# A token tower layer in fp32r on one core: scores in four strips, stationary router weights, a new order of the instruction lists, and the first block's sums over positions by identity matmuls

## The reference

```python
h = take(table, x)                                   # (8, 1024, 256)
h = h + attn(layernorm(h))                           # 16 heads of 16, over the FIRST axis: 8 positions
h = h + ffn(layernorm(h))
# attn: q, k, v = x @ Wqkv.T + b; softmax(q k / 4) over the 8 positions; out = (p v) @ Wo.T + bo
# ffn: s = sigmoid(x @ Wg.T), 16 experts in 4 groups; the best 2 groups, in them the best 4 experts,
#      their s normalised, times 2.5; out = sum_e w_e * relu(x @ W1[e].T)^2 @ W2[e].T
#      + relu(x @ Ws1.T)^2 @ Ws2.T                   # hidden 128 per expert, 256 shared
```

## Time and profile before

| what | value |
|---|---|
| median of 3 runs | 1297.22 us (1296.58 to 1298.70) |
| the profiled execution | 1296.51 us, span from first to last instruction 1294.7 us |
| granted TensorE clock, mean | 0.995 |
| TensorE busy | 1259.3 us, 97% |
| VectorE busy | 1022.7 us, 79% |
| ScalarE busy | 591.2 us, 46% |
| GpSimd busy | 500.2 us, 39% |
| DMA | 91.66 MB, 71 GB/s in the mean |

### The profile page before, as it was taken

One profiled execution on the slowest core, in us unless ns is written; L12 is line 12 of the kernel. 1 busy time (PEld: TensorE's weight loads), 2 busy tenths in 40 slices (PEclk: granted clock), 3 DMA queues, 4 the chain that ended last, 5 costly groups with the idle time before them and its releaser, 6 DMA issues.

```text
span 1294.7 us, 19965 instructions
## 1 busy us (share of the span) xinstructions
PE 1259.3 (97%) x7556; PEld 1037.6 (80%) x7556; DVE 1022.7 (79%) x1732; ACT 591.2 (46%) x1040; POOL 500.2 (39%) x717
## 2 busy tenths in 40 slices
PE   4798999999999999999999999999999999999998
PEld 3467889797888979788797888979788797888987
DVE  4989787887878789787878878788787878978754
ACT  5234445444554544454353544544355354444443
POOL 6437254161623507253260724416262360705100
PEclk9899999999999999999999999999999999999999
DMA  6002222121321212122121322212122120212131
GB/s 217 1 17 83 66 83 82 35 82 49 99 66 55 94 33 97 52 83 82 34 86 45 100 66 82 71 46 82 50 89 76 51 92 29 94 49 83 66 107 57
DMA packets 34128, 91.66 MB, mean 71 GB/s; under 512 B 4720, under 2 KB 13296, under 8 KB 34032
## 3 DMA queue, kind: packets, MB, share of 16 engines
q1 hardware_dynamic: 30960, 81.99, 19.0%
q0 software_dynamic: 3072, 8.39, 2.5%
HBM read 81.46 MB, written 8.91 MB: 70 GB/s over the span
## 4 chain that ended last, share of the span: by engine, by line
PE 94%; DVE 3%; issue 1%; ACT 1%; POOL 1%; DMA 0%; DVEq 0%; POOLq 0%; SPq 0%
PE psY L1157 32%; PE psH L1142 30%; PE psB L1188 10%; PE psB L1203 9%; PE psA L1233 4%; PE psB L1221 2%; PE psA L1221 2%; PE psA L1245 2%; PE psB L1174 1%; PE psA L1174 1%; DVE ring L771 1%; PE psA L1254 1%; PE psY L1261 0%; DVE stats L754 0%; POOL xin L399 0%
## 5 line engine op out<-in xcount | busy, mean ns | idle before, releaser
L1157 PE MATMUL psY<-w_hi,hid_hi 128*128 128x256 f32 x1152 | 328.5, 285 | 0.0
L1157 PE MATMUL psY<-w_hi,hid_lo 128*128 128x256 f32 x1152 | 324.5, 282 | 0.0
L1157 PE MATMUL psY<-w_lo,hid_hi 128*128 128x256 f32 x1152 | 323.6, 281 | 0.0
L733 DVE SCALAR_TENSOR_TENSOR r_sb<-psH,cwB 128x512 f32<-128x512 f32 x256 | 174.8, 683 | 113.7 <-PE psH L1142 102.9
L533 ACT ACTIVATE hid_hi<-r_sb 128x512 fp32r<-128x512 f32 x288 | 179.8, 624 | 181.4 <-PE psY L1157 181.4
L1157 PEld LDWEIGHTS psY<-w_hi,hid_hi 128*128 128x128 f32 x1152 | 217.3, 189 | 31.4 <-issue 23.5
L1142 PE MATMUL psH<-xT_hi,w_hi 128*128 128x512 f32 x576 | 229.2, 398 | 1.4 <-DVE r_sb L733 1.4
L1142 PE MATMUL psH<-xT_hi,w_lo 128*128 128x512 f32 x576 | 227.4, 395 | 0.0
L1142 PE MATMUL psH<-xT_lo,w_hi 128*128 128x512 f32 x576 | 227.3, 395 | 0.0
L531 ACT ACTIVATE p_sb<-r_sb 128x512 f32<-128x512 f32 x288 | 180.2, 626 | 101.8 <-DVE r_sb L733 94.6
L1157 PEld LDWEIGHTS psY<-w_lo,hid_hi 128*128 128x128 f32 x1152 | 216.9, 188 | 8.1
(11 more groups left out here) (136 smaller groups left out, 1980.6 us busy)
## 6 DMA issues: line engine op xcount, KB each, us to landing
cwB<-cw_dram SPq DMA_DIRECT2D x128, 512.0 KB, 3.9
out<-h SPq DMA_DIRECT2D x32, 256.0 KB, 3.2
xin<-table,idx POOLq DMA_INDIRECT x64
ring<-w_t SPq DMA_DIRECT2D x4, 256.0 KB, 5.3
h<-w_t SPq DMA_DIRECT2D x2, 512.0 KB, 8.5
ring<-w_t SPq DMA_DIRECT2D x1, 512.0 KB, 5.9
p_sb<-w_t SPq DMA_DIRECT2D x2, 256.0 KB
cwB<-w_t SPq DMA_DIRECT2D x1, 512.0 KB
```

The costliest lines, as they stand in the source:

```text
L733: nc.vector.scalar_tensor_tensor(r_sb[:, n % 2, :], psH[:, n % 2, :], 0.0, cwB[:, (r // QN) % 2, r % QN, :], ALU.max, ALU.mult).then_inc(w ...
L1157: last = nc.tensor.matmul(psY[:, j // 2, (j % 2) * D:(j % 2 + 1) * D], hid[a][:, e % R, j * P:(j + 1) * P], W2[b][:, e, :], start=(e == 0 ...
```

## The change

It has five parts.

1. **Scores.** A slot's number now is t = 2 lp + ih, and `score(blk, lp)` issues the four strips of both halves in one go: four matmuls into four different strips of 32 partitions. There are four calls of it in place of eight, in a period in two groups, (0, 1) and (2, 3), as there were two groups of four slots before.
2. **Router.** The router's weights, high and low, and Wo's high part share one tile. `logits` loads 128 columns of it (32 of the router, 96 of Wo whose results nobody reads) and streams the tokens: 4 matmuls of 512 columns. The result, 32 x 512, is copied out by ScalarE (`logits_out`, into cwT, which now has 32 rows), and `logits_back` brings it with 4 transposes to where `router` reads it.
3. **Sums of block 0.** For blk == 0 the sum over the key positions is made by `part_sum`: eight f32 matmuls with the identity, added up in psY, which the experts don't use yet. `attention_hi`/`_lo` of block 0 read psY. VectorE and GpSimd have no sums for block 0. In later blocks nothing changes here.
4. **Start part.** The second gather goes to right behind the first, ahead of the constants and of rstd_of(0, 0); warm groups, weight pieces and the calls of blocks 0 and 1 are laid out anew on all four lists.
5. **Periods.** The calls are the same but for the new ones, in a new order on TensorE, VectorE and ScalarE; on GpSimd only bias_in moves up.

The core of the diff:

```diff
         W2 = [sb(f"w2_{p}", [P, X_ALL, D], f32r) for p in ("hi", "lo")]
         WQKV = [sb(f"wqkv_{p}", [P, KH, 6, P], f32r) for p in ("hi", "lo")]
-        WO = [sb(f"wo_{p}", [P, KH, D], f32r) for p in ("hi", "lo")]
-        WG = sb("wg_hi_lo", [P, KH, 2, E], f32r)
+        WGO = sb("wg_hi_lo_wo_hi", [P, KH, 2 * E + D], f32r)
+        WO = [WGO[:, :, 2 * E:2 * E + D], sb("wo_lo", [P, KH, D], f32r)]
 
...
 
-        SUMS_VECTOR = ((1, 3, 5, 7), (3, 7))
+        SUMS_VECTOR = (3, 7)
 
         QKV_ORDER = [(0, 0), (1, 0), (0, 1), (1, 1), (2, 0), (2, 1)]
         QKV_SB = [q_sb, k_sb, v_sb]
@@ -272,7 +275,7 @@
         def product_on(eng, ns, blk, t):
 
 
-            lp, ih = t % LP, t // LP
+            lp, ih = t // KH, t % KH
             if lp == 0:
                 eng.wait_ge(qkv_ready, nth(blk, 6, 2 * (ih + 1)))
             if blk == 0 and t == 0:
@@ -289,13 +292,14 @@
 
         def summer(blk, t):
 
-            on_vector = t in SUMS_VECTOR[min(blk, 1)]
-            mine = [u for u in range(SLOTS) if (u in SUMS_VECTOR[min(blk, 1)]) == on_vector]
-            before = sum(1 for b in range(blk) for u in range(SLOTS) if (u in SUMS_VECTOR[min(b, 1)]) == on_vector)
-            return int(on_vector), before + mine.index(t), mine.index(t)
+            on_vector = t in SUMS_VECTOR
+            mine = [u for u in range(SLOTS) if (u in SUMS_VECTOR) == on_vector]
+            return int(on_vector), (blk - 1) * len(mine) + mine.index(t), mine.index(t)
 
         def wait_sum(eng, blk, t):
-            if blk >= 0:
+            if blk == 0:
+                eng.wait_ge(part_mm, t + 1)
+            elif blk > 0:
                 who, k, _at = summer(blk, t)
                 eng.wait_ge(o_ready[who], k + 1)
 
...
                     gather(b + 3)
+                if b + 2 < B:
+                    bias_in(b + 2)
                 if b + 1 < B:
                     root_of_sum(b + 1)
                 if b + 2 < B:
                     sum_of(b + 2, 0)
                     sum_of(b + 2, 1)
-                    bias_in(b + 2)
 
             link(nc.gpsimd.memset(half_neg[:, :], -0.5))
             link(nc.gpsimd.memset(ident[:, :], 0.0))
...
 
+            gather_first(1)
+            rstd_of(0, 0)
             constants_small()
-            rstd_of(0, 0)
             constants_spread()
-            gather_first(1)
             rstd_of(0, 1)
-            sum_of(0, 0)
             bias_in(0)
-            sum_of(0, 2)
-            sum_of(0, 4)
-            sum_of(0, 6)
             rstd_of(1, 0)
             gather(2)
+            bias_in(1)
             root_of_sum(0)
             sum_of(1, 0)
             sum_of(1, 1)
-            bias_in(1)
             for b in range(B + 1):
                 period(b)
...
                 wait(act, h_mm, (blk - 1) * X_ALL)
-                nc.scalar.copy(xT2[blk % 2][0][:, ih, :], o_sb[:, ih, :]).then_inc(o_hi, 1)
+                src = psY if blk == 0 else o_sb
+                nc.scalar.copy(xT2[blk % 2][0][:, ih, :], src[:, ih, :]).then_inc(o_hi, 1)
+
+            def logits_out(blk):
+                act.wait_ge(logit_mm, nth(blk, 1, 1))
+                wait(act, cwT_stored, nth(blk, 16, 0))
+                nc.scalar.copy(cwT[:, :], psA[0:2 * E, 0, :]).then_inc(lgT_ready, 1)
 
             def router(blk):
-                act.wait_ge(logit_mm, nth(blk, 1, 1))
+                act.wait_ge(lg_back, nth(blk, 1, 1))
                 wait(act, route_step, nth(blk, ROUTE_STEPS, 0))
                 nc.scalar.copy(lg[:, :, :, :].rearrange("p a b c -> p (a b c)"),
-                               psA[:, 0, 0:TT * 2 * E]).then_inc(lg_ready, 1)
+                               psA[:, 1, 0:TT * 2 * E]).then_inc(lg_ready, 1)
...
@@ -1190,19 +1209,21 @@
                                                 stop=(kh == KH - 1 and (a, b) == PASSES[-1]))
                 last.then_inc(qkv_mm, 1)
 
-            def score(blk, t):
-
-                lp, ih = t % LP, t // LP
-                pe.wait_ge(prod_ready[ih], nth(blk, LP, lp + 1))
-                if t == 0:
+            def score(blk, lp):
+
+                for ih in range(KH):
+                    pe.wait_ge(prod_ready[ih], nth(blk, LP, lp + 1))
+                if lp == 0:
                     if blk == 0:
                         pe.wait_ge(const_step, CONST_SMALL)
                     pe.wait_ge(qkv_ready, nth(blk, 6, 5))
-                for li in range(2):
-                    row = 64 * ih + 32 * li
-                    last = nc.tensor.matmul(psB[row:row + 32, 0, :], head_sum[:, lp, :], ring[:, t % 4, li, :],
-                                            start=(lp == 0), stop=(lp == LP - 1))
-                last.then_inc(score_mm, 1)
+                for ih in range(KH):
+                    for li in range(2):
+                        row = 64 * ih + 32 * li
+                        last = nc.tensor.matmul(psB[row:row + 32, 0, :], head_sum[:, lp, :],
+                                                ring[:, (KH * lp + ih) % 4, li, :],
+                                                start=(lp == 0), stop=(lp == LP - 1))
+                    last.then_inc(score_mm, 1)
 
             def spread_probs(blk, t):
 
...
@@ -1222,6 +1243,16 @@
                                             start=True, stop=True)
                 last.then_inc(spread_mm, 1)
 
+            def part_sum(t):
+
+                pe.wait_ge(av_ready, t + 1)
+                a = ring[:, t % 4, :, :].rearrange("p l (m n) -> p l m n", m=L)
+                ih, lp = t // LP, t % LP
+                for m in range(L):
+                    last = nc.tensor.matmul(psY[:, ih, 2 * lp * NN:(2 * lp + 2) * NN].rearrange("p (l n) -> p l n", l=2),
+                                            ident[:, :], a[:, :, m, :], start=(m == 0), stop=(m == L - 1))
+                last.then_inc(part_mm, 1)
+
             def out_projection(blk):
                 if blk == 0:
...
                 pe.wait_ge(xT_lo[1], nth(blk, 1, 1))
                 x = xT2[blk % 2]
+                for kh in range(KH):
+                    for a in range(2):
+                        last = nc.tensor.matmul(psA[:, 0, :], WGO[:, kh, 0:P], x[a][:, kh, :],
+                                                start=(kh == 0 and a == 0), stop=(kh == KH - 1 and a == 1))
+                last.then_inc(logit_mm, 1)
+
+            def logits_back(blk):
+                pe.wait_ge(lgT_ready, nth(blk, 1, 1))
                 for j in range(TT):
-                    for kh in range(KH):
-                        for a in range(2):
-                            last = nc.tensor.matmul(psA[:, 0, j * 2 * E:(j + 1) * 2 * E],
-                                                    x[a][:, kh, j * P:(j + 1) * P],
-                                                    WG[:, kh, :, :].rearrange("p a e -> p (a e)"),
-                                                    start=(kh == 0 and a == 0), stop=(kh == KH - 1 and a == 1))
-                last.then_inc(logit_mm, 1)
+                    last = nc.tensor.transpose(psA[:, 1, j * 2 * E:(j + 1) * 2 * E], cwT[:, j * P:(j + 1) * P],
+                                               ident[0:2 * E, 0:2 * E])
+                last.then_inc(lg_back, 1)
 
             def weights_transpose(blk):
                 pe.wait_ge(route_step, nth(blk, ROUTE_STEPS, ROUTE_STEPS))
```

More of the change, by code:

```diff
@@ L626, in period @@
                     square(b, 8)
+                    square(b, 9)
                 if b + 2 < B:
@@ L639, in period @@
                     qkv_out(b + 2, 2)
+                    qkv_out(b + 2, 3)
+                if b + 1 < B:
+                    logits_out(b + 1)
                 if b < B:
-                    square(b, 11)
                     square(b, 12)
+                if b + 2 < B:
+                    qkv_out(b + 2, 4)
                 if b + 1 < B:
@@ L972, in period @@
                 if b < B:
-                    hidden_lo(b, 11)
+                    weigh(b, 12)
+                if b + 2 < B:
+                    product(b + 2, 2)
+                    product(b + 2, 3)
+                if b < B:
                     hidden_lo(b, 12)
@@ L1005, in period @@
                 if b + 1 < B:
-                    route(b + 1, 10)
+                    route(b + 1, 5)
+                    route(b + 1, 6)
+                    route(b + 1, 7)
+                    route(b + 1, 8)
+                if b < B:
+                    weigh(b, 14)
+                if b + 1 < B:
+                    route(b + 1, 9)
+                if b < B:
+                    hidden_lo(b, 13)
+                    weigh(b, 15)
+                if b + 1 < B:
+                    route(b + 1, 10)
+                if b < B:
+                    hidden_lo(b, 14)
+                if b + 1 < B:
+                    route(b + 1, 11)
+                if b + 2 < B:
+                    scores_max(b + 2)
+                if b < B:
+                    hidden_lo(b, 15)
+                if b + 1 < B:
+                    route(b + 1, 12)
```

(76 more changed lines are left out.)

251 lines of the change are left out of this document (113 added, 138 removed).

## The result

The changed kernel takes **1253.85 us** (1252.72 to 1255.35, four runs) against 1296.9 for the kernel before in the same session: a ratio of 0.9667, 95% interval 0.965 to 0.9683, so 43 us or 3.3% faster. Forecast were 1248 and a range of 1240 to 1264. The profiled execution took 1255.35 us, span 1253.6; it is the longest of the four, and the others' spans are 1251.0 to 1251.8.

The account below looks back on a forecast made before the run. TensorE's work was taken to bound each period. Span 1294.7 - 52.4 (14 periods) + 1.5 (leftover waits) + 2.3 (b = 14) - 0.5 (start) = 1245.6, hence 1248 us median; forecast 1242 to 1254, wider range 1240 to 1264.

Parts of the forecast that it names:

- Scores, 3.44 a period: Scores on TensorE: two groups a period, each in four four-record waves instead of eight pairs, 1.72 us less per group.
- Router, 0.3: Router on TensorE: four long matmuls plus four transposes, 1.47 to 1.5 us instead of 1.79, so 0.3 less.
- Work of a period, 73.3: TensorE's work in a full period: 77.07 less 3.44 and 0.3, giving 73.3 us; VectorE keeps 10.8 of slack.
- Order of a period: TensorE's new list: narrowest from transpose_rows to logits, 3.68 us given against 3.51 needed; 0.1 a period added for leftover waits.
- b = 14, 2.3 longer: Block 14: router saves 0.3, but waits of 1.4 before the transposition and 1.2 before the logits add 2.6.
- The start, -0.5 net: Start plus first period: up(0, 3) 1.6 us later, 2.1 fewer waits in the first period; bounds -4 and +7.
- The value of the identity matmuls: Block 0's sums in the start: identity matmuls end at about 66.6 us, against 67.26 for the last VectorE sum before.
- R4: Start 6 us worse through partial sums or gather: 1254; no separate chance, at the end of the range given 0.72.
- R1: New waits of 1 us or so in each period, at the logits, spread_probs or weights' transpose: 1262; chance 0.18.
- R2: Scores: only pairs overlap, so four-strip waves cost two steps and save nothing: 1296, no change; chance 0.02.
- R3: Period is a ring of waits, not TensorE's work; it stays and the route adds 1.4: 1319; chance 0.02.

Follow-up runs that it names:

- both edits of bias_in: Changed kernel with GpSimd's bias_in moved back behind the two sums, in the periods and in the start part: 1246.67 us, ratio 0.9608.

## Why the prediction was right, and where it was off

- **Scores, 3.44 a period: right.** From the twelve records of the start a step of 0.43 for four strips was read; a group of 16 takes 1.92, 1.71 less, twice 3.42.
- **Router, 0.3: right**, 0.33 alone. The change of tiling mode that the Trainium skill speaks of (TensorEngine Tiling (Array Packing), Key Properties) costs about 0.1 on either side of the transposes, not 0.2, and a small transpose 0.06.
- **Work of a period, 73.3: a little less**, 73.15 without the collision. The scores and the router are 3.75 of the 3.92 us; where the other 0.17 comes from no run here shows. Over the periods of b = 1 to 13 it is 2.3 us that the forecast didn't have.
- **Order of a period: the narrowest place was named right**, transposition to logits with 0.2 to spare, and it is the one that fails, by 0.52 (73.67 against 73.15). I allowed 0.1. The mechanism was not the one I had in mind: I had counted bias_in's move at nothing and had not asked what VectorE does in those 2.4 us. It costs twelve full periods 0.52 and the first about as much: b = 0 to 13 are 6.6 us longer than in the trace with bias_in behind the sums in the periods.
- **b = 14, 2.3 longer: right**, 2.1, and the two waits are the ones named, as the run that removes them shows.
- **The start, -0.5 net: off by 5.5, the largest miss.** up(0, 3) is at 107.93, not 103.3, and the first period 4.9 shorter instead of 5.7 (3.74 and 2.1, less the 0.1 allowed). So start and first period together are 1.4 longer where the forecast has them 4.1 shorter. Of the steps: normalise(0, 0) at 17.7 (forecast 2 to 3.3 later, 2.4 measured); scores_max at 41.20, not 40.4; a part_sum 7.30 / 4 = 1.8 as taken; residual at 72.98, not 71.1, for 24 projection matmuls have to wait for attention_lo at 69.70; route 0 at 91.84, not 88.0, of which 2.4 are the product stopped by bias_in; and then the 7 us at half the granted clock, 2.6. The prediction has no term for the clock. With both edits of bias_in the two together are at 179.76, 2.3 above the forecast.
- The value of the identity matmuls was put at almost nothing; it is 6 us, the additions' length and the clock of what follows.
- **The sum** was 1245.6 of span; the profiled one is 1253.6, 8 more: 5.5 the start with the first period, 2.7 the periods of b = 1 to 13 (the collision, less the work that came out lower), -0.3 b = 14. The others' spans are 1251 to 1252; they have no windows.
- **Where the time fell.** The forecast was 1242 to 1254, and 1253.85 is at its very end. R4 had 1254 there, through a start 6 us worse by the partial sums or the gather. The start is nearly that much worse, but mostly by the stopped product and the clock; the partial sums are a gain. That R4's number fits is luck. The time is also in the range of R1, 1248 to 1262, with one wait of half a microsecond instead of several. What holds by its mechanism is the 44.6 us of the periods of b = 1 to 13, forecast as 47.3.
- R2 is refuted: four steps for sixteen records. So is R3: the period is 3.9 shorter with VectorE's busy time no less, 62.97 against 62.52.

## What to carry to other kernels

When TensorE has no gap in a period, its list can be costed by counting starts, and the hard part of a prediction is the margins at its waits. For every instruction that is moved on GpSimd, look at which VectorE instructions with both inputs in SBUF will run beside it: here one move of a 2.4 us instruction that nobody waits for cost 7 us. A start part has to be costed with the granted clock of each stretch, as TensorE's waits in it decide what the work behind them costs. And when the last rounds of a loop lack part of its work, their distances have to be counted for themselves.

## What the runs showed of the hardware

- f32 matmuls into four different strips of 32 partitions run side by side at the step of one, 0.43 us (16 records in 1.92 us, against 3.63 with two strips). With eight records for two strips ahead of the first for the other two it is still four steps, 1.94 us.
- An SBUF-to-SBUF VectorE instruction of 0.69 us that began 0.51 ahead of a GpSimd instruction of 2.38 took 3.45. Beside bias_in's new place this happened in thirteen periods. A product of 1.22 that began 0.17 ahead of it took 3.64.
- After 8 us in which TensorE was busy for 1.4, 24 matmuls ran at a granted clock of 0.50 and took 5.26 us instead of 2.92. After 3 us in which it was busy for 0.81 it ran 7 us at 0.51; where it had been busy for 2.08 of the same 3 us, at 1.00.
